# Moving the low halves of the keys to GpSimd and the scaling of the attention weights to VectorE, with six heads of eight split instead of four

## The reference, cut to what matters

```python
# B, S = 64, 32;  D, HQ, HK = 128, 32, 8;  16 pages of 32 cached keys;  SCALE = 1/sqrt(128)
q = rope(rmsnorm((x @ Wq.T).reshape(B, S, HQ, D)))
k = rope(rmsnorm((x @ Wk.T).reshape(B, S, HK, D)))
v = (x @ Wv.T).reshape(B, S, HK, D)
k_all = concat([k_cache[block_table], k])      # 512 cached and 32 new keys in each batch
v_all = concat([v_cache[block_table], v])
scores = einsum('bqhd,bkhd->bhqk', q, k_all) * SCALE       # 4 query heads share a key head
probs  = softmax(where(valid, scores, -1e30))
out    = einsum('bhqk,bkhd->bqhd', probs, v_all).reshape(B, S, HQ * D) @ Wo.T
```

## Time and profile before

| what | value |
|---|---|
| time, median of 3 runs | 2404.17 us (2403.21 to 2405.09) |
| the profiled execution | 2405.73 us, span 2403.6 us |
| PE busy in the span | 2279.4 us (95%) |
| DVE busy | 1793.8 us (75%) |
| ACT busy | 1302.3 us (54%) |
| POOL busy | 1167.9 us (49%) |

### The profile page before, as it was taken

One profiled execution on the slowest core, in us unless ns is written; L12 is line 12 of the kernel. 1 busy time (PEld: TensorE's weight loads), 2 busy tenths in 40 slices (PEclk: granted clock), 3 DMA queues, 4 the chain that ended last, 5 costly groups with the idle time before them and its releaser, 6 DMA issues. The chain is left out here.

```text
span 2403.6 us, 52557 instructions
## 1 busy us (share of the span) xinstructions
PE 2279.4 (95%) x16384; PEld 1970.0 (82%) x16384; DVE 1793.8 (75%) x3555; ACT 1302.3 (54%) x2627; POOL 1167.9 (49%) x1246
## 2 busy tenths in 40 slices
PE   4869899999998599999999999999999997999999
PEld 4858677777776599999999999999999997788887
DVE  6654399999998588888888888888888886432221
ACT  2652588888887355555555555555555554421111
POOL 3420144444444477767777677777767774000000
PEclk7989999999999799999999999999999999999999
DMA  5563333333322788888888888888888885743442
GB/s 224 204 214 99 88 110 108 97 103 109 109 88 83 234 295 294 292 294 276 285 292 291 288 295 289 278 292 293 292 291 294 276 285 185 248 123 101 127 140 61
DMA packets 451704, 501.65 MB, mean 209 GB/s; under 512 B 95653, under 2 KB 390565, under 8 KB 443302
## 3 DMA queue, kind: packets, MB, share of 16 engines
q1 hardware_dynamic: 414758, 366.37, 47.6%
q0 software_dynamic: 36864, 134.23, 15.9%
HBM read 404.02 MB, written 96.47 MB: 208 GB/s over the span
## 5 line engine op out<-in xcount | busy, mean ns | idle before, releaser
L1103 POOL TENSOR_TENSOR att_probs<-att_probs,att_inverse 128x512 f32<-128x512 f32 x512 | 535.3, 1046 | 290.0 <-DVE att_inverse L1299 285.6
L1207 ACT ACTIVATE att_probs<-att_probs,att_low 128x544 f32<-128x544 f32 x512 | 383.8, 750 | 515.6 <-DVE att_low L1286 448.4
L1164 PE MATMUL att_o<-att_probs_t,att_values 128*128 128x128 f32 x4096 | 540.9, 275 | 0.0
L1286 DVE CUSTOM_DVE_ANT_0 att_probs<-att_score,att_mask,att_batch_cols 128x544 f32<-128x544 f32 x512 | 399.6, 780 | 140.0 <-PE att_score L1129 100.7
L1164 PEld LDWEIGHTS att_o<-att_probs_t,att_values 128*128 128x128 f32 x4096 | 497.7, 192 | 0.0
L1295 DVE COPY att_probs_t<-att_turn 128x512 f32<-128x512 f32 x512 | 350.4, 684 | 1.2 <-PE att_turn L1144 1.2
L1089 POOL DMA_INDIRECT att_values<-L_cond_v_cache,att_v_rows_of x256 | 282.2, 1103 | 82.4 <-POOL att_v_rows_of L1085 49.9
L1129 PE MATMUL att_score<-att_keys_raw,att_queries_raw 128*128 128x288 f32 (+1 forms) x1024 | 290.9, 407 | 28.9 <-DMA att_queries_raw<-q_t 26.7
L1144 PE MATMUL att_turn<-ident,att_probs 128*128 128x128 f32 x2048 | 311.3, 275 | 1.2 <-POOL att_probs L1103 0.8
L798 PE MATMUL proj_proj<-x3t_hi,proj_w_hi 128*128 128x512 f32 x640 | 266.9, 417 | 6.9 <-DVE proj_w_lo L858 6.9
L1144 PEld LDWEIGHTS att_turn<-ident,att_probs 128*128 128x128 f32 x2048 | 244.3, 141 | 32.9 <-POOL att_probs L1103 1.4
(11 more groups left out here) (128 smaller groups left out, 3986.8 us busy)
## 6 DMA issues: line engine op xcount, KB each, us to landing
att_keys_raw<-L_cond_k_cache SPq DMA_DIRECT2D x1024, 128.0 KB
q_t<-proj_q_out SPq DMA_DIRECT2D x32, 1024.0 KB, 3.9
att_queries_raw<-q_t SPq DMA_DIRECT2D x64, 512.0 KB
o_t<-att_heads_out SPq DMA_DIRECT2D x64, 512.0 KB, 6.5
out_o_raw<-o_t SPq DMA_DIRECT2D x32, 1024.0 KB, 5.7
front_adapters<-L_cond_weight SPq DMA_DIRECT2D x16, 1024.0 KB, 10.9
w_nat<-L_cond_Wq SPq DMA_DIRECT2D x8, 1024.0 KB, 5.3
v_new<-values_v_out SPq DMA_DIRECT2D x64, 128.0 KB, 2.0
```

Source lines behind the costliest of these rows:

```text
L1103: nc.gpsimd.tensor_tensor(probs[:, k, 0:L], probs[:, k, 0:L], inverse[:, k:k + 1].to_broadcast([P, L]), ALU.mult).then_inc(probs_ready, 1)
L1164: last = nc.tensor.matmul(o, values[j][:, t, h * D:(h + 1) * D], probs_t[m % 2][:, t * P:(t + 1) * P], start=(t == 0), stop=False, skip_gr ...
L1207: nc.scalar.activation(probs[:, k, :], probs[:, k, :], ACT.Exp, bias=low[k][:, 0:1], scale=-1.0, accum_out=total[k][:, 0:1]).then_inc(exp_ ...
L1286: nc.vector.tensor_tensor_reduce(out=probs[:, k, :], in0=score_ps[:, LEFT:LEFT + KEYS], in1=mask[j][:], scale=batch_cols[j][:, h:h + 1], s ...
```

## The change

GpSimd and VectorE swap two tasks. The low halves of keys and queries are now subtracted on POOL, and the weights are scaled on DVE. DVE scales by one tensor_scalar with the reciprocal as its scalar, one head late: `normalise(n - 1)` in the turn of head n, after `main_part(n - 2)`. `NATIVE` falls from 4 to 2, so that six heads of a batch are split. The pieces have 576 elements (five), 384 (one), and 768 for the queries. ACT begins with them in head 1 of the batch before, POOL in head 2, and the queries' low half falls to head 0 of the batch itself. The keys' loads are issued after head 2's scores, since `NATIVE` sets that too. `columns` moves from head 4 to head 1.

```diff
-    NATIVE = 4
-    ACT_FROM, DVE_FROM = 4, 5
+    NATIVE = 2
+    ACT_FROM, POOL_FROM = 1, 2
...
-    PARTS = [slice(0, 3), slice(3, 6), slice(6, 9), slice(9, 13), slice(13, NPP + 1)]
+    PARTS = [slice(0, 3), slice(3, 6), slice(6, 9), slice(9, 12), slice(12, 15), slice(15, NPP + 1)]
...
 (POOL)
+            def split(b, c, v):
+                pool.wait_ge(hi_ready, b * (NP + 1) + (c + 1))
+                if c < NP:
+                    nc.gpsimd.tensor_tensor(keys_lo[v][:, PARTS[c]], keys_raw[v][:, PARTS[c], NATIVE:HK], f32(keys_hi[v][:, PARTS[c]]),
+                                            ALU.subtract).then_inc(lo_ready, 1)
+                else:
+                    nc.gpsimd.tensor_tensor(queries_lo[v][:], queries_raw[v][:, NATIVE:HK], f32(queries_hi[v][:]),
+                                            ALU.subtract).then_inc(lo_ready, 1)
...
                         load((j + 1) % 2, i * 2 + (j + 1), h - 3)
-                    pool.wait_ge(inverse_ready, i * N + n + 1)
-                    k = n % RING
-                    nc.gpsimd.tensor_tensor(probs[:, k, 0:L], probs[:, k, 0:L], inverse[:, k:k + 1].to_broadcast([P, L]),
-                                            ALU.mult).then_inc(probs_ready, 1)
-                    if n % GH == GH - 1:
-                        (new_group, the same on gpsimd)
+                    if HK - POOL_FROM + h <= NP:
+                        split(i * 2 + j, HK - POOL_FROM + h, j)
+                    if h >= POOL_FROM and not (last_pair and j == 1):
+                        split(i * 2 + (j + 1), h - POOL_FROM, (j + 1) % 2)
...
 (DVE)
-            def invert(i, n):
+            def normalise(i, n):
+                m = n % N
+                k = m % RING
                 dve.wait_ge(exp_done, i * N + (n + 1))
-                nc.vector.reciprocal(inverse[:, n % RING:n % RING + 1], total[n % RING][:]).then_inc(inverse_ready, 1)
+                nc.vector.reciprocal(inverse[:, k:k + 1], total[k][:]).then_inc(inverse_ready, 1)
+                dve.wait_ge(inverse_ready, i * N + (n + 1))
+                nc.vector.tensor_scalar(probs[:, k, 0:L], probs[:, k, 0:L], inverse[:, k:k + 1], None, ALU.mult).then_inc(probs_ready, 1)
+                if m % GH == GH - 1:
+                    heads = slice(k - GH + 1, k + 1)
+                    nc.vector.tensor_tensor(new_group[m // GH % 2][:], probs[:, heads, L:KEYS],
+                                            inverse[:, heads].unsqueeze(2).to_broadcast([P, GH, S]), ALU.mult).then_inc(group_ready, 1)
...
                         main_part(i, n - 2)
-                    if HK - DVE_FROM + h <= NP:
-                        split(i * 2 + j, HK - DVE_FROM + h, j)
-                    ...
-                    invert(i, n)
+                    if n >= 1 or not first:
+                        normalise(i, n - 1)
+                    if h == 1 and not (last_pair and j == 1):
+                        dve.wait_ge(scores_masked, i * N + j * HK)
+                        columns(i * 2 + (j + 1), (j + 1) % 2)
```

More of the change, by code:

```diff
@@ L1100, in pair @@
                         load((j + 1) % 2, i * 2 + (j + 1), h - 3)
-                    pool.wait_ge(inverse_ready, i * N + n + 1)
-                    k = n % RING
-                    nc.gpsimd.tensor_tensor(probs[:, k, 0:L], probs[:, k, 0:L], inverse[:, k:k + 1].to_broadcast([P, L]),
-                                            ALU.mult).then_inc(probs_ready, 1)
-                    if n % GH == GH - 1:
-                        heads = slice(k - GH + 1, k + 1)
-                        nc.gpsimd.tensor_tensor(new_group[n // GH % 2][:], probs[:, heads, L:KEYS],
-                                                inverse[:, heads].unsqueeze(2).to_broadcast([P, GH, S]), ALU.mult).then_inc(group_ready, 1)
+                    if HK - POOL_FROM + h <= NP:
+                        split(i * 2 + j, HK - POOL_FROM + h, j)
+                    if h >= POOL_FROM and not (last_pair and j == 1):
+                        split(i * 2 + (j + 1), h - POOL_FROM, (j + 1) % 2)
             for t in range(PPT):
                 load(0, 0, t)
+            for c in range(HK - POOL_FROM):
+                split(0, c, 0)
             pair(0, True, False)
@@ L1258, in _ @@
         def _(dve):
[L1259 to L1266, removed]
             def columns(b, v):
@@ L1306, in pair @@
                         main_part(i, n - 2)
-                    if HK - DVE_FROM + h <= NP:
-                        split(i * 2 + j, HK - DVE_FROM + h, j)
-                    if not (last_pair and j == 1):
-                        if h >= DVE_FROM:
-                            split(i * 2 + (j + 1), h - DVE_FROM, (j + 1) % 2)
-                        elif h == DVE_FROM - 1:
-                            dve.wait_ge(scores_masked, i * N + j * HK)
-                            columns(i * 2 + (j + 1), (j + 1) % 2)
-                    invert(i, n)
+                    if n >= 1 or not first:
[3 more added lines that the diff above has]
+                        columns(i * 2 + (j + 1), (j + 1) % 2)
             dve.wait_ge(pages_loaded, 16)
@@ L1324, in _ @@
             columns(0, 0)
-            for c in range(HK - DVE_FROM):
-                split(0, c, 0)
             pair(0, True, False)
@@ L1331, in _ @@
             main_part(PAIRS, -2)
+            normalise(PAIRS, -1)
             main_part(PAIRS, -1)
```

## The result

The change made the kernel slower: 2537.99 us (2537.05 to 2539.52) against 2403.69 (2400.24 to 2405.09), ratio 1.0561 with a 95% interval of 1.0548 to 1.0575. The forecast was 2560, range 2420 to 2610.

What follows compares the result with a forecast made beforehand. PE's own work and the handshake of scores and mask were taken to bound attention jointly. 2405.7 + 156 for longer batches + 2 for the first batch, less 1.6, gave 2562, rounded to 2560 us; range 2420 to 2610.

Steps and rivals of the forecast that it cites:

- What bounds; the gain of the split: Attention: PE's work and the scores-mask handshake tie; two more split heads gain 0.35 us a batch, 22 us in all.
- The scaling's place on the path: DVE's turn: scaling starts at mask +1.50, takes 0.49; weights ready at +1.99, next mask possible at +1.91.
- The late chain: PE's transposes wait 0.25 us in a plain split head for weights scaled one turn later; without contention +31 us.
- POOL's prices: POOL's subtraction pieces take 1.40 (576 elements), 0.99 (384) and 1.80 us (768); by the cheaper slope 1.15, 0.83 and 1.47.
- The port: DVE's scaling, requested while POOL subtracts, waits until POOL ends, because their shared port pair is an exclusive lock.
- The walk: One attention batch followed mask by mask, with scaling waits of 0.48 to 0.80: 21.32 us instead of 18.89.
- the cheap end: POOL's pieces by the cheaper slope: a batch of 20.24 us, 86 us more in all, time 2492.
- The sum: Whole kernel: 2405.7 + 156 + 2 = 2564 us, less 1.6 for the median: 2562.
- a part that I had left alone: Attention batch: 0.18 us of loop ends and small waits, beyond the 18.89 that the spacings explain.
- The first batch: Three more ACT copies ahead of the first softmax cost about 2 us, with 0 to 8 possible.
- Rival 4: POOL's gathers stretched by DVE's two-port instructions in heads 4 to 6: 79 us more, 2640; chance 0.08.
- Rivals 2 and 3: Attention: no scaling contention, only late transposes, about 2436, chance 0.13; or only PE's shorter heads count, 2382, chance 0.09.

Runs made afterwards that it cites:

- f1_tiny_order: e1_tiny with POOL's order exchanged in heads 3 to 6, subtraction first and gather after it; 2443.99 us, ratio 1.0168.
- f2_swap_clean: Changed kernel with the engines' swap kept but four heads split, pieces and heads of ACT's and POOL's work as before the change; 2451.42 us, ratio 1.0201.
- e4_six_only: Kernel before the change with six heads split, engines' tasks unswapped, so DVE subtracts the larger pieces; 2483.31 us, ratio 1.0333.
- e1_tiny: Changed kernel with each of POOL's subtractions cut to 32 elements, low halves otherwise zero; 2476.39 us, ratio 1.0304.
- e7_accum: Changed kernel with the scaling in a tensor_scalar form that also writes an accumulator nobody reads; 2564.58 us, ratio 1.0663.
- e3_swap_only: Changed kernel with four heads split instead of six, the rest of its schedule not moved; 2518.49 us, ratio 1.0469.
- f4_reordered: Changed kernel reordered: PE's product before transposes, DVE's scaling before copying, POOL's pieces after the scaling, in seven key pieces; 2519.64 us, ratio 1.0478.
- e2_half: Changed kernel with each of POOL's subtractions cut into two of half the heads, one behind the other; 2619.66 us, ratio 1.0899.
- e5_late: Changed kernel with everything after the scaling (transposes, copy, product) one turn later; 2710.72 us, ratio 1.1275.

## Why the prediction was right, step by step

- *What bounds; the gain of the split.* The forecast allowed 22 us. No run shows it whole: f1_tiny_order is 7 us faster than f2_swap_clean, and the split alone cost 79 (e4_six_only), since DVE's pieces grew and waited for POOL. The bound "nothing else changed" was never met.
- *The scaling's place on the path.* Forecast at mask +1.50, measured +1.49 (1214.91 against 1213.42), and 0.49 long. Right in most heads; in head 4 it is +1.71, where the walk had +1.57.
- *The late chain.* Forecast +31 with the port free; f1_tiny_order shows +40, f2_swap_clean +47 with four heads split. Right in mechanism, the total a little small. The place was only half right: the forecast had PE wait 0.25 in each plain split head, and in f2_swap_clean PE is late by 0.26 and 0.22 in heads 4 and 6, by 0.14 in head 0, and not at all in heads 5 and 7.
- *POOL's prices.* 1.40, 0.99 and 1.80 were forecast; 1.43 and 1.82 were measured, and for 384 elements 1.01 alone (f2_swap_clean) and 1.21 in the changed kernel, where this piece waits for a scaling. The row with two full operands was the right one; the cheap end fell. That POOL would wait was not in the sum.
- *The port.* The mechanism is shown from two sides: POOL's subtractions cut short, the scaling is back at 0.49 (e1_tiny, f1_tiny_order); in the form that doesn't wait, it is steady beside POOL (e7_accum). The size was off. The walk gave waits of 3.25 us a batch; 512 instructions at a mean of 0.803 instead of 0.487 make 2.53. A scaling that waited ended 0.29 after POOL, where the walk had let it begin at POOL's end and take the full 0.49: 0.2 too much in each of five heads. Against that, POOL was still busy for 3.57 us a batch when the five scalings were requested, not for 3.25. Two errors of opposite sign left 0.7 too much.
- *The walk.* It gave 21.32 for a batch; 21.11 was measured. Masks follow each other from head 0 on at 2.44, 2.55, 2.66, 2.79, 2.80, 2.50, 3.10 and 2.28; the walk had 2.59, 2.58, 2.63, 2.71, 2.88, 2.50, 3.18 and 2.25. That it came this near is in part luck: of the 0.7 too much wait only 0.2 reached the batch, since in heads 5 and 6 other work ended the head and in head 4 the scaling was requested later than walked.
- *The sum.* The 24 us between 2562 and 2538 are two terms. The batch was 0.21 shorter than walked (13 us). And the walk was set against 18.89, while before took 19.04 after its first batch: a part that I had left alone counted as a loss (10 us).
- *The first batch.* Forecast 2 us, measured 4.4 - 2.07 = 2.4. After it the loads of keys stayed hidden.
- *Rival 4, stretched gathers.* It did not happen: the median gather takes 0.96, shorter than the 1.00 to 1.18 of the earlier trace rows. The reason given was misread. The gather of 1.12 at 1202.79 did not run alone, since a subtraction of DVE ran on 0.26 into it; the one of 1.00 ran beside neither that nor a mask-making, and 1.18 is 0.18 longer. In the changed kernel a gather behind a piece begins when the scaling has 0.13 left. Gathers do stretch: to 1.16 beside a whole scaling in e3_swap_only, and to 1.52 beside DVE's subtractions in e4_six_only. The size that the prediction quotes stands on that page of the Trainium skill, "SBUF — State Buffer", not in the box but in the section "A bandwidth-pool intuition that's wrong (but worth ruling out)".
- *Rivals 2 and 3.* The late chain alone is where the two kernels with a free port and the schedule in order lie (2444 and 2451, rival 2 at 2436). Nothing came near 2382.

## What to carry to other kernels

When two engines swap work, price not the work but the moment: the same scaling hardly held PE up on POOL in its own turn. On DVE one turn late it came with a loss of 40 to 47 us, and with 94 more where it met POOL's instructions. Look for an instruction whose minimum and maximum lie far apart, and compare its end with the other engine's end; a constant difference names what it waits for. A list of waits by releaser can name the wrong heads: check by head whether the waiting engine lost anything. When a chain is turned to remove a wait, follow it round to where it closes, as f4_reordered did not.

## What the runs showed of the hardware that was not expected

- A tensor_scalar that waited for POOL ended 0.29 or 0.30 us after POOL's instruction, not 0.49: a part of its own time had passed during the wait.
- Back-to-back instructions of POOL mostly kept the scaling out as one long one (e2_half, up to 2.24 us for a scaling; e5_late, 3.84), but not always: in head 6 of after it got in between two each time.
- What began first by the profile did not always go first: a subtraction of DVE that began 0.12 before POOL's scaling ended 0.63 after it (e4_six_only).
- The accumulating form took 0.747 us with or without POOL beside it, the plain one 0.49 to 1.65.
- POOL's gathers took 0.96 after the change, and 1.00 to 1.18 before it; next to a scaling that began 0.13 earlier 1.17 (e1_tiny), next to subtractions of DVE up to 1.52 (e4_six_only).
- In e1_tiny, scores that ended during such a gather reached DVE up to 1 us late. Exchanging gather and subtraction removed this; through what the signal is held up no run here shows, and nothing like it is in the trace of after.
